# A gated cross-attention and expert kernel: from batch 4 three taps' similarities are spread abreast, two PSUM uses share a bank, and the expert means are summed on POOL

## The reference

```
def xattn(feature, embedding, weight):              # per batch: C = 128 channels, T = 1024 columns
    sim = stack([cos(emb, emb shifted left), cos(emb, emb), cos(emb, emb shifted right)])   # 3 x T
    att = repeat(sim, C, axis=1)                    # one similarity row per row of the unfolded input
    inp = stack([pad(feature)[:, :, k:k + T] for k in range(3)], axis=2).reshape(B, 3 * C, T)
    return einsum('bit,oi->bot', inp * att, weight.reshape(O, 3 * C))

def ffn(x):                                         # tokens = the 128 rows of a batch, D = 1024
    logits = x @ router_w.T + router_b              # 8 experts, the two best, softmax weights
    h = einsum('nd,erd->ner', x, A)                 # first layer, 8 x 16 = 128 columns
    return einsum('ner,eor->no', h * w[:, :, None], Bm) * SCALING

x = x + tanh(g_xattn) * xattn(layernorm(x), ctx, W)
x = x + tanh(g_ffn) * ffn(layernorm(x))
```

## Time and profile before

| | |
|---|---|
| median of three runs | 232.0 us (231.58 to 232.76) |
| the profiled execution | 230.52 us |
| span of its records | 228.7 us |
| PE, DVE, ACT, POOL busy, share of the span | 90%, 73%, 63%, 68% |

### The profile page before, as it was taken

How to read it: one execution, slowest core, us unless ns; L and a number is a source line. 1 busy time by engine, 2 the same in 40 slices (tenths; PEclk the granted TensorE clock), 3 DMA queues, 4 the chain that set the end, 5 groups by cost and what they waited for, 6 DMA issues and landing times.

```text
span 228.7 us, 3793 instructions
## 1 busy us (share of the span) xinstructions
PE 206.3 (90%) x1116; PEld 132.2 (58%) x1116; DVE 166.3 (73%) x403; ACT 145.1 (63%) x253; POOL 154.9 (68%) x277
## 2 busy tenths in 40 slices
PE   5898959676999999979899999989899999999963
PEld 5564335444675554747566555747566767767741
DVE  1178968196699876296899875395999797886752
ACT  3588948729579976528388966438386867633310
POOL 2351618957669999638669999539579988868340
PEclk9999999999999999999999999999999999999999
DMA  6799503406122453422222222022222402020224
GB/s 207 262 350 385 229 0 133 147 0 229 48 92 92 158 212 108 171 92 93 92 95 92 93 93 95 0 92 92 92 96 92 160 25 95 1 92 0 95 92 183
DMA packets 8883, 27.28 MB, mean 119 GB/s; under 512 B 1632, under 2 KB 2240, under 8 KB 8864
## 3 DMA queue, kind: packets, MB, share of 16 engines
q1 hardware_dynamic: 8432, 26.78, 31.2%
q10 hardware_dynamic: 432, 0.26, 0.4%
HBM read 18.65 MB, written 8.39 MB: 118 GB/s over the span
## 4 chain that ended last, share of the span: by engine, by line
PE 63%; DVE 20%; issue 7%; POOL 5%; DMA 2%; ACT 1%; POOLq 0%; DVEq 0%; ACTq 0%
PE bank L852 10%; PE bank L877 10%; PE bank L804 7%; PE bank L838 7%; DVE pt L661 6%; PE bank L866 5%; PE bank L856 4%; PE bank L857 4%; PE bank L858 4%; DVE x L668 3%; PE bank L895 3%; PE bank L896 2%; PE bank L897 2%; POOL pt_lo L362 2%; DMA et<-ctx 2%
## 5 line engine op out<-in xcount | busy, mean ns | idle before, releaser
L362 POOL TENSOR_TENSOR pt_lo<-pt,pt_hi 128x512 fp32r<-128x512 f32 x60 | 76.8, 1284 | 38.3 <-ACT pt_hi L484 32.2
L661 DVE TENSOR_TENSOR pt<-xn,bank 128x512 f32<-128x512 f32 x96 | 64.1, 671 | 9.8 <-PE bank L838 4.0
L484 ACT ACTIVATE pt_hi<-pt 128x512 fp32r<-128x512 f32 x60 | 37.7, 629 | 47.3 <-DVE pt L661 47.0
L838 PE MATMUL bank<-rows,sel 96*128 96x512 bf16 x96 | 36.5, 387 | 5.0 <-DVE pt L661 3.3
L877 PEld LDWEIGHTS bank<-aT,xT 128*128 128x128 f32 x256 | 34.1, 190 | 8.0 <-ACT xT L490 4.1
L852 PE MATMUL bank<-pt,wT 128*128 128x512 f32 x72 | 37.5, 602 | 0.0
L877 PE MATMUL bank<-aT,xT 128*128 128x136 f32 x256 | 35.1, 280 | 1.1 <-ACT xT L490 1.1
L856 PE MATMUL bank<-pt_hi,w_hi 128*128 128x512 f32 x60 | 28.1, 468 | 0.0
L838 PEld LDWEIGHTS bank<-rows,sel 96*128 96x128 bf16 x96 | 9.1, 97 | 32.8 <-issue 17.3
L668 DVE TENSOR_TENSOR x<-bank,xt 128x512 f32<-128x512 f32 x32 | 21.9, 685 | 7.9 <-PE bank L852 7.9
L705 DVE TENSOR_TENSOR x<-bank,x 128x512 f32<-128x512 f32 x32 | 21.7, 679 | 6.6 <-PE bank L897 6.6
(11 more groups left out here) (96 smaller groups left out, 349.8 us busy)
## 6 DMA issues: line engine op xcount, KB each, us to landing
et<-ctx SPq DMA_DIRECT2D x16, 512.0 KB, 6.5
xt<-x SPq DMA_DIRECT2D x16, 512.0 KB, 3.3
out<-x SPq DMA_DIRECT2D x15, 512.0 KB, 2.6
aT_in<-expert_aT SPq DMA_DIRECT2D x1, 544.0 KB, 10.8
bm_in<-expert_b SPq DMA_DIRECT2D x1, 512.0 KB, 10.5
out<-x SPq DMA_DIRECT2D x2, 256.0 KB, 2.1
sel<-select SPq DMA_DIRECT2D x1, 216.0 KB, 11.3
wT_in<-conv_wT SPq DMA_DIRECT2D x1, 192.0 KB, 5.7
```

The lines of the kernel that those rows point to most:

```text
L362: nc.gpsimd.tensor_tensor(pt_lo[:, i, :], pt[:, i, :], pt_hi[:, i, :], ALU.subtract).then_inc(lo_done, 1)
L484: nc.scalar.activation(pt_hi[:, i, :], pt[:, i, :], ACT.Copy).then_inc(hi_done, 1)
L661: nc.vector.tensor_tensor(pt[:, i, :], xn[:, n % 2, h * HALF + t:(h + 1) * HALF + t], sim_ps[k % 2][:, :], ALU.mult).then_inc(mod_done, 1)
L838: nc.tensor.matmul(sim_ps[k % 2][:, :], sel[:, SLOT_OF[n], t, :], rows[:, q % 2, half(h)], start=True, stop=True).then_inc(spread, 1)
```

## The change

Five things are changed.

1. From batch 4 on (`ABREAST`), the three similarity rows that a half of a batch needs are spread by three matmuls in succession, each with nine rows at partitions 0, 32 and 64 (row groups of the array), into three banks: 0, 1 and 4. Their operands are the new tiles `sel3` and `rows3`. `rows3` has two buffers, by batch, and is filled by nine SP DMAs for each batch, each from three partitions of `rows` to three of `rows3` (6 KB). The leads change with it: DVE modulates taps 0 and 1 of a half in one step and tap 2 in the next.
2. Bank 4 is taken from the token transposes, which share bank 6 with the experts' first layer. So `experts_in` waits for both halves' evacuation, and `transpose_tokens(n, 0)` waits for `logit_done` of batch `n - 1`.
3. On PE `tap(m)` now comes ahead of `experts_in` and of `transpose_tokens(n, 0)`; on DVE `pick_experts` moves a step ahead, and the norms' second and third part on PE come earlier (`NEIGHBOURS`, `ROWS`).
4. The expert matrix's eight parts are summed on POOL (three adds) and averaged by one fp32 matmul.
5. The three setup DMAs of ACT move to SP, the order of the first loads changes, and `WARM_UP` goes from 7 to 11.

The diff, cut to its core:

```diff
-WARM_UP = 7
+WARM_UP = 11
+ABREAST = 4
-NEIGHBOURS = {(0, 4): 1, (2, 3): 2, (6, 3): 3, (10, 3): 4}
-ROWS = {(0, 5): 1, (3, 0): 2, (7, 0): 3, (11, 0): 4}
+NEIGHBOURS = {(0, 4): 1, (2, 0): 2, (6, 0): 3, (10, 0): 4}
+ROWS = {(0, 5): 1, (2, 2): 2, (6, 2): 3, (10, 2): 4}
-        sim_ps = bank[0:2]
+        sim_ps = (bank[0], bank[1], bank[4])
-        xT_ps = bank[4]
-        h_ps = bank[6]
+        xT_ps = h_ps = bank[6]
         def modulated(m):
+            if m >= STEPS * ABREAST - 3:
+                return min(m + 4 - m % 3 // 2, M - 1)
         def spread_by(m):
+            if m >= STEPS * ABREAST - 3:
+                return min(m - m % 3 + 5, M - 1)
+        def loads3(n):
+            return 48 * (n // 2 - ABREAST // 2 + 1)
...
+            def load_rows3(n):
+                q, b = GROUP_OF[n], SLOT_OF[n]
+                sp.wait_ge(rows_left_done, q + 1)
+                sp.wait_ge(rows_rest_done, q + 1)
+                if n >= ABREAST + 2:
+                    sp.wait_ge(spread, STEPS * (n - 1))
+                for t in range(TAPS):
+                    for f in range(TAPS):
+                        sp.dma_start(rows3[32 * t + TAPS * f:32 * t + TAPS * (f + 1), n % 2, :],
+                                     rows[32 * f + b:32 * f + b + 9:4, q % 2, :]).then_inc(rows3_in[n % 2], 16)
             for n in range(1, B):
                 if n >= 4:
                     store(n - 4)
                 if n + 3 < B:
                     load_x(n + 3)
...
+                if ABREAST <= n + 1 < B:
+                    load_rows3(n + 1)
...
+            def sum_means():
+                pool.wait_ge(aT_in_done, 16)
+                nc.gpsimd.tensor_tensor(aT_sum[:, :, :], aT_in[:, 0:4, :], aT_in[:, 4:8, :], ALU.add).then_inc(summed_means, 1)
...
             def modulate(k):
-                dve.wait_ge(spread, k + 1)
+                dve.wait_ge(spread, k + 1 if n < ABREAST else k - t + TAPS)
...
             def spread_similarities(k):
+                if n >= ABREAST:
+                    if t:
+                        return
+                    pe.wait_ge(rows3_in[n % 2], 3 * loads3(n))
+                    pe.wait_ge(mod_done, k)
+                    for m in range(TAPS):
+                        nc.tensor.matmul(sim_bank(k + m)[:, :], sel3[32 * m:32 * m + 9, m, :],
+                                         rows3[32 * m:32 * m + 9, n % 2, half(h)], start=True, stop=True).then_inc(spread, 1)
+                    return
...
             def transpose_tokens(n, h):
+                if h == 0 and n >= 1:
+                    pe.wait_ge(logit_done, n)
             def experts_in(n, h):
-                if h == 0 and n >= 1:
-                    pe.wait_ge(logit_done, n)
-                pe.wait_ge(xT_out, 2 * n + h + 1)
+                pe.wait_ge(xT_out, 2 * n + 2)
...
-                if n == 0 and i == 1:
+                tap(m)
+                if n == 0 and i == 3:
                     expert_means()
-                tap(m)
+                if i == 2 and n >= 1:
+                    experts_in(n - 1, 0)
+                if i == 3 and n >= 1:
+                    experts_in(n - 1, 1)
+                if i == 5:
+                    transpose_tokens(n, 0)
```

75 lines of the change are left out of this document (46 added, 29 removed).

## The result

| | median us | range | span of the profiled execution | mean granted clock |
|---|---|---|---|---|
| before | 231.8 | 231.4 to 232.8 | 228.7 | 1.00 |
| changed kernel | 289.6 | 288.9 to 292.5 | 290.6 (an execution of 292.5) | 0.91 |

The changed kernel is 25% slower: ratio 1.251, 95% interval 1.243 to 1.259. The direction was forecast, the size was not: 290 lies far above the range of 227 to 254.

A forecast was written before the change was run, and what follows sets the result against it. PE bounds the kernel before; afterwards a ring through DVE, ACT and PE does. 228.7 - 2.6 + 0.7 + 4.8 + 4.4 + 4.5 = 240.5 us of span, forecast as 243.5 measured, range 227 to 254.

The forecast's parts named there:

- The late ring: Closed loop of waits through DVE, ACT and PE in late batches: 11.7 us a batch, against 10.1 before.
- S to A: From the issue of step 3's spread to that of the next step 0's spread: 4.72 us.
- A to S: From the issue of step 0's spread to that of step 3's spread: 7.0 us.
- The walk: One late batch of the new order followed through the engines with durations from the trace: 11.7 us, 0.4 either way.
- The nine DMAs: Spread in step 3 waits for SP's rows3 copies: 0.5 us a batch in batches 4 to 12, +4.5 (0 to 15).
- The upper bound of 0.43: SP's issue time per rows3 DMA at most 0.43 us, giving a wait of 1.6 in nine batches, 15 us.
- The third rival: Slower by SP: nine DMAs issued at 0.43 and landing in 2.1 us; more than 249 us, chance 0.15.
- Batches 4 to 11: Eight batches at 11.7 us plus context work on the ring: 105.8 us against 101.4 before, +4.4.
- The gain of the row groups: On PE, three spreads abreast take 0.42 us against 0.69, which gains 0.54 us a batch.
- the charge of 0.1 at each change of shape: PE loses 0.1 us whenever matmuls change tiling shape; without this charge a batch would gain 0.92.
- Setup, -2.6: Before the batches: expert means shrink, -1.7 us, and the first context sum runs at the higher clock, -0.9.
- the first rival: Faster: PE stays the bound and each wait is absorbed; 223 us, whole way 218 to 230.8, chance 0.25.

The follow-up runs named there:

- hidden_first: rows3_early with ACT's hidden_out of step 4 written ahead of feature_squares; 255.2 us, late period 11.77.
- finish_one: sums_first with DVE's finish(n - 3, 1) written ahead of the two products of step 3; 248.8 us.
- finish_first: rows3_early with the moves of hidden_first and sums_first, the residual ahead of step 0's products, both finish calls ahead of their steps' products; 237.5 us.
- rows3_early: The changed kernel with the nine rows3 DMAs at the head of SP's round, ahead of store and load of x; 260.3 us.
- sums_first: rows3_early with ACT's sums_evacuate ahead of pt_hi and feature_squares in batches 1, 5 and 9; 250.8 us.
- tidy_serial: tidy with the three spreads of 96 rows one after the other from rows, without rows3, sel3 and the nine DMAs; 232.9 us.
- tidy: finish_first with the norms of groups 3 and 4 two steps later, and on ACT tokens_evacuate ahead of normalize in step 1; 229.9 us.

## Why the prediction was right and wrong

**The late ring, 11.7 us: right, by half of its cause.** Measured 11.75 to 11.78, S to A 4.83 and A to S 6.95. The walk with durations of the trace held to 0.1 us in both parts, and that is partly luck. It stopped at the first chain that was long enough. hidden_first, finish_one and finish_first show that `finish` behind two products, in the bank that the hidden transpose shares, is a second chain of equal length. Batch 14, which was put 0.5 us shorter for its missing `feature_squares`, took 11.76 like the others. The prediction had named that bank only for `experts_out` in A to S.

**The nine DMAs, 4.5 us (0 to 15): wrong, this is the term that failed.** The step was "it carries a fortieth of the bytes, so I take the lower values": 0.33 an issue. Measured 0.68. (Its own 0.33 gives A + 2.6 + 9 x 0.33 + 1.7 = A + 7.3, not the 7.5 written.) With 0.68 the prediction's own sum gives A + 2.6 + 0.34 + 6.2 + 1.1 = A + 10.2, a wait of 3.2 over A + 7.0, 29 us in nine rounds. Measured: S at A + 10.16 to A + 11.56, and 29.3 us by rows3_early. That the two totals meet is partly chance: the nine waits are 2.5 us on average and not 3.2, since the context work had lengthened A to S in some rounds, and the wait in batch 3 and the lower clock behind the waits make up the rest. The landing (1.14, against 1.7 to 2.1 from the earlier trace rows) was overestimated. The upper bound of 0.43 came from rows of large loads, and it was not even the longest issue in the trace of the kernel before. In the setup SP issues two constants of 4 KB each:

```profile
8.43 1.29 SPq L302 DMA_DIRECT2D ids<-expert_ids  x1
9.77 0.86 SPq L303 DMA_DIRECT2D rb<-router_b  x1
```

Two loads of 0.5 KB took 0.43 and 0.44 us there. So few bytes did not mean a short issue there either, and these lines should have widened the range upwards; why the two took so long no run shows. The third rival named this mechanism, with a price half of the true one.

The Trainium skill, "DMA: Bandwidth & Descriptors", Issuing engines are not separate DMA queues, says that the sequencer's time to initiate a DMA is usually small relative to the DMA itself. For these copies the trace does not agree: 0.68 us of issue each, against 1.14 us from the last issue to the spread, and 6.16 us for the nine. The rule to coalesce small transfers (same page, Rules for kernel authors), which the prediction had put beside the sum, was the better guide: the same bytes in three DMAs instead of nine (dmas_three) took 264.3 us instead of 289.6.

**Batches 4 to 11, 105.8 us: wrong.** Even without DMA waits they took 121.0 (A at 75.55 and 196.55 in rows3_early). Of the 15.2 missing, 9.7 are the two waits for `sums`, by sums_first (111.3). The walk had been made for a late batch and the context work laid on top as durations: squares, sums, norms. `transpose_context` behind a spread is not a duration but a closed loop (spread, product, `pt_hi`, `sums`, PE). The rest is 5.5, read from sums_first. The norms brought A to S to 10.04 and 10.18 us against 6.97, together 6.3 and not 4.4; the squares, sums and rows made the other rounds 10.7 us longer and not 7.4. The start of batch 4 (75.55 in rows3_early, about 3 us later than the sum has it, of which 2.6 are the setup) and the batches from 12 on (some 3 us) are the small remainder.

**The gain of the row groups, 0.54 us a batch: too large.** The three do overlap: together they last 0.39 us, as long as one alone, so their starts lie within 0.1 us. But the charge of 0.1 at each change of shape came on top of 0.33 for the three, not of 0.22: 0.10 + 0.33 + 0.11 is 0.54 for each three where 0.42 was taken, and three with 96 rows one after the other cost 0.65 and not 0.69; a batch gains 0.25 (tidy_serial less tidy). The Trainium skill, "TensorEngine Tiling (Array Packing)", names the drain in Key Properties, and the trace agrees with 0.10 and 0.11. By its Theoretical Speedup the gain had been estimated at 0.92 a batch; 0.25 was measured.

**Setup, -2.6: the steps right, the sum wrong.** The first context sum takes 0.99 instead of 1.94, the means 0.33 instead of 1.85, and the total is unchanged (1.000). The gain was counted at its own place, and the prediction did not ask what is late next (DVE's `simp`), and no term stood for a lower clock behind a longer wait.

**The clock** stood in no term. Behind DMA waits PE was granted the lower level of its clock for a time (0.62 over 236.28 to 239.60). From S to A the granted clock was 0.56 to 0.71 in eight of ten rounds of the profiled execution, and 1.00 behind the two shortest waits (0.69 us). Five of the eight, batches 3, 4, 8, 11 and 12, were 1.0 to 2.0 us longer from S to A than in rows3_early. Batches 5 and 9 hold the wait for `sums` as well, and rows3_early has 0.68 and 0.69 there without any DMA wait.

**Rivals and chances.** The case with nearly all waits absorbed exists: it is tidy, 229.9, inside the first rival's 218 to 230.8. But it needs the DMAs in another place and seven moves in the engines' order that the change did not make. Its crucial question, whether the logit is there 3.7 us after S and `finish` 2.8 after A, was the right one.

In sum: 289.6 = 229.9 for the tidy order, plus 29.3 for the DMAs behind `load_x`, 9.5 for `sums_evacuate`, 4.0 for hidden pass and residual, 9.3 for `finish`, and 7.6 for norms and `xT`. The last four come in the order in which they were taken away; since chains lie side by side, another order would share them out otherwise. They are also differences between medians of different chips: by the ratios to the kernel before they are 10.5, 4.0, 7.8 and 8.2.

## What to carry to other kernels

When single operations are bundled (here three spreads), every engine's order must be walked again, since what was spread over three steps is now needed and freed at once. Look for all chains that arrive at the same instant, not for one that suffices: a single move that brings nothing refutes only that it is alone. And a kind of instruction that no row of the trace shows has no bound from rows of another kind; price it by a probe before a ring of waits is built on it, and count issues, not bytes.

## What the runs showed of the hardware

- Small copies inside SBUF cost SP 0.60 to 0.77 us each to issue, for 1 to 16 rows; a load of 128 rows from HBM 0.34 (L302). The spread that waited for nine of them started 1.14 us after the last issue.
- Three matmuls of 9 rows and 512 columns in three row groups take 0.33 us together, plus 0.10 to enter and 0.11 to leave; 96 rows one after the other take 0.47 plus 0.18 behind them. Where PE is full, the difference is 0.125 us.
- From S to A, behind DMA waits of 1.94 to 4.08 us, PE's granted clock was 0.56 to 0.71 in eight rounds of one execution, two of which also hold a wait for `sums`; it was 1.00 behind two waits of 0.69 us. With ten filler matmuls in the wait it was 1.00 in seven of nine rounds; the other two have the wait for `sums`.
- A setup in which the second tap starts 1.9 us earlier ends no earlier: PE idled 2.33 us instead of 1.32 ahead of 30.75 us, and its granted clock was 0.57 between 30 and 38 us. Whether the first caused the second is open.
